# The end of attention re-ordered in a fused modulation, attention and feed-forward kernel: weight loads divided, first feed-forward sample moved a slot, first sample's values moved

## The reference, cut to what matters

```python
h = layernorm(x, gamma1, beta1)
Q, K, V = (h @ Wq + bq), (h @ Wk + bk), (h @ Wv + bv)      # 16 heads of 32
scores = einsum('bhqd,bhkd->bhqk', Q, K) / sqrt(32)        # causal mask, then softmax
x1 = x + softmax(scores) @ V @ Wo + bo
h2 = layernorm(x1, gamma2, beta2)
ff = gelu(h2 @ W1 + b1) @ W2 + b2                          # 512 -> 2048 -> 512
out = x + g * (x1 + ff - x)
```

## Time and profile before

| | |
|---|---|
| median of 3 runs | 1770.07 us (1762.8 to 1770.21) |
| the profiled execution's own time | 1769.55 us |
| its span | 1767.8 us |
| mean granted TensorE clock | 0.976 of full speed |
| TensorE busy | 1669.0 us, 94% of the span |
| VectorE / ScalarE / GpSimd busy | 66% / 56% / 24% |
| attention, slots 0 to 31 | about 278 to 1029 us of the span |

### The profile page before, as it was taken

The page is one execution under the profiler, slowest core; times in us unless marked ns, Lnnn a source line. Parts: engine busy times, 40 slices in busy tenths (PEclk is TensorE's granted clock), DMA queues, the critical chain, the costliest instruction groups (busy, mean ns, idle before and its releaser), DMA issues.

```text
span 1767.8 us, 27388 instructions
## 1 busy us (share of the span) xinstructions
PE 1669.0 (94%) x9384; PEld 1336.3 (76%) x9384; DVE 1174.1 (66%) x2758; ACT 986.7 (56%) x2289; POOL 420.2 (24%) x638
## 2 busy tenths in 40 slices
PE   5799997899999999999999879999999999999999
PEld 3688765667676767776676648888899999999998
DVE  5899776676676767676766555867665656565643
ACT  4788743777676766776667573634343434342422
POOL 6688520313131221313131122010101010101010
PEclk8999998899999999999999989999999999999999
DMA  6122233333434434343333713486646464646451
GB/s 281 72 95 75 94 116 99 97 96 96 106 94 112 105 83 117 97 120 83 93 96 73 240 54 110 160 302 263 249 167 239 167 247 163 259 166 255 162 197 66
DMA packets 61827, 254.82 MB, mean 144 GB/s; under 512 B 10580, under 2 KB 15956, under 8 KB 45944
## 3 DMA queue, kind: packets, MB, share of 16 engines
q1 hardware_dynamic: 61688, 253.06, 43.8%
HBM read 153.93 MB, written 48.23 MB: 114 GB/s over the span
## 4 chain that ended last, share of the span: by engine, by line
PE 72%; DVE 12%; ACT 6%; DMA 4%; SPq 3%; issue 2%; POOL 1%; DVEq 0%; ACTq 0%; POOLq 0%
PE psum L82 20%; PE psum L83 19%; PE psum L84 19%; PE psum L1616 3%; PE psum L1599 3%; PE psum L1644 3%; DVE psum L1147 2%; ACT psum L1384 2%; DMA k_stack<-k_maxima 1%; SPq L914 1%; ACT k_exps L1394 1%; SPq L922 1%; DMA k_stack<-k_samples 1%; ACT k_samples L1411 1%; DVE k_samples L1188 1%
## 5 line engine op out<-in xcount | busy, mean ns | idle before, releaser
L1384 ACT ACTIVATE psum<-psum,b_mx 128x512 f32<-128x512 f32 (+3 forms) x512 | 260.6, 511 | 227.0 <-DVE b_mx L1147 225.1
L1147 DVE CUSTOM_DVE_ANT_0 psum<-psum,b_mask 128x512 f32<-128x512 f32 (+3 forms) x512 | 247.8, 505 | 206.8 <-PE psum L1599 203.9
L2443 ACT ACTIVATE k_act<-k_stack_f,k_smalls 128x512 f32<-128x512 f32 x112 | 81.0, 723 | 336.1 <-DVE k_stack_f L2231 336.1
L1394 ACT ACTIVATE k_exps<-psum 128x512 f32<-128x512 f32 (+1 forms) x384 | 205.3, 536 | 10.8 <-PE psum L1616 10.8
L1616 PE MATMUL psum<-k_stack 98*128 98x512 f32 (+3 forms) x512 | 158.2, 351 | 32.7 <-ACT k_exps L1394 18.0
L2084 POOL TENSOR_SCALAR k_result<-k_result,k_pb 128x512 f32<-128x512 f32 x32 | 59.9, 1887 | 455.4 <-DVE k_result L2150 455.4
L2210 DVE TENSOR_TENSOR k_act_lo<-k_act,k_act_hi 128x512 fp32r<-128x512 f32 x112 | 77.4, 691 | 130.2 <-ACT k_act_hi L2446 130.1
L1599 PE MATMUL psum<-k_stack 96*128 96x512 f32 (+3 forms) x512 | 159.6, 354 | 1.4 <-ACT psum L1384 1.4
L82 PE MATMUL psum<-k_act_hi,k_w_hi 128*128 128x512 f32 x384 | 150.9, 393 | 1.0 <-DVE k_act_lo L2210 0.6
L83 PE MATMUL psum<-k_act_lo,k_w_hi 128*128 128x512 f32 x384 | 150.6, 392 | 0.0
L84 PE MATMUL psum<-k_act_hi,k_w_lo 128*128 128x512 f32 x384 | 150.3, 391 | 0.0
(11 more groups left out here) (365 smaller groups left out, 4568.9 us busy)
## 6 DMA issues: line engine op xcount, KB each, us to landing
k_stack<-w_factors SPq DMA_DIRECT2D x35, 1792.0 KB, 7.3
k_stack<-k_samples SPq DMA_DIRECT2D x384, 128.0 KB, 2.4
k_weights<-w_factors SPq DMA_DIRECT2D x17, 1792.0 KB, 7.8
x<-k_tokens SPq DMA_DIRECT2D x10, 1024.0 KB, 3.9
k_tokens<-x SPq DMA_DIRECT2D x8, 1024.0 KB, 4.8
d<-k_result SPq DMA_DIRECT2D x32, 256.0 KB, 2.5
k_raw<-x SPq DMA_DIRECT2D x8, 1024.0 KB, 4.8
k_raw<-d SPq DMA_DIRECT2D x8, 1024.0 KB, 6.9
```

The costliest lines, as they stand in the source:

```text
L1147: last = dve.tensor_tensor_reduce(got, got, mask[:, S - width:S], -INV_SQRT_DH, -2.0 * MASKED, ALU.add, ALU.min, mx[n % 2][:, h, t:t + 1])
L1384: act.activation(sc(n, u)[:, at:at + width], sc(n, u)[:, at:at + width], ACT.Exp, bias=mx[n % 2][:, h, t:t + 1], scale=-1.0, accum_out=sum ...
L1394: act.activation(exps[n % 2][:, h, at:at + width], by_key(n, u)[:, 0:width], ACT.Exp, scale=INV_SQRT_DH).then_inc(k_act, 1)
L2443: act.activation(act_f[:], whole_tile, ACT.Gelu, bias=small(smalls, "b1", 2 * pair % M + second)).then_inc(pair_gelu, 1)
```

## The change

It moves instructions between places of the lists; no instruction of the arithmetic is added or removed. In its parts:
1. **Values of sample 0.** The second half of its values (24 matmuls) goes from slot 1 to slot 0 (`values_in`). In slots 0 and 1 the first `maxima` stands at step 7, not 8, and `maxima_out` one step earlier too (`maxima_step`).
2. **Steering.** VectorE takes the four steering products at steps 5 and 6, two each, instead of three at step 6 and one at step 7.
3. **SyncE, every sample.** In slots with g = 0 and g = 1 the small copies of the maxima (`max_rows(n, 0)`) go ahead of the 1 MB store of the steered sample and of the 1 MB load of the next.
4. **SyncE, the last slots.** The loads of sample 0's `x` and `d` go from the end of slot 29 to two places in slot 30. The W1 and W2 loads of slot 30 go behind the maxima: W1's first half into slot 31, W2's quarter to the end of slot 31, W1's second half into slot 32.
5. **The first feed-forward sample.** `tokens_back`, the scaling and splitting, the weight splits and the first two `first_product` go from slots 32 (end) and 33 into slot 32; what follows moves a slot forward too. Four second products then stand ahead of the last output products of attention, which before lay between them. The additions for sample 0 are made at steps 2 and 3 of slot 31 instead of 0 to 3.

The core of the diff (left out: the steps of `split_low`, `scale_back` and of the later `step(m)`, which move in the same way):

```diff
+def maxima_step(n):
+    return 8 if n >= 2 else 7
 def values_in(n):
     b, g = divmod(n, G)
-    if n == -1:
-        return 0, V_TILES[0]
-    return b, (V_TILES[g] if present(b) and g < 2 and (b or g) else ())
+    if n in (-1, 0):
+        return 0, V_TILES[n + 1]
+    return b, (V_TILES[g] if present(b) and g < 2 and b else ())
...
         def slots(after):
...
+                if n == GROUPS - 2:
+                    first_after("x2")
+                if n in (GROUPS - 1, GROUPS):
+                    after("w1", n - GROUPS + 1)
                 if 0 <= n + 1 < GROUPS:
                     stack_rows(n + 1, (0, 1))
...
+                if g == 3 and present(b - 1):
+                    attention_out(b - 1, 3)
+                if 0 <= n < GROUPS:
+                    max_rows(n, 0)
+                if n == GROUPS - 2:
+                    first_after("d")
+                if n == GROUPS - 1:
+                    after("w2")
                 if g == 0 and present(b + 1):
                     steered_out(b + 1)
                 if g == 1 and present(b + 2):
                     sample_in(b + 2)
-                if n == GROUPS - 2:
-                    after("weights")
-                if g == 3 and present(b - 1):
-                    attention_out(b - 1, 3)
-                if 0 <= n < GROUPS:
-                    max_rows(n, 0)
...
-                if u == 6:
-                    for j in range(J - 1):
-                        steered(b + 1, j)
-                if u == 7:
-                    steered(b + 1, J - 1)
+                if u in (5, 6):
+                    steered(b + 1, 2 * (u - 5))
+                    steered(b + 1, 2 * (u - 5) + 1)
...
-            if n == GROUPS and u in (10, 11):
-                tokens_back(AFTER, 2 * (u - 10))
-                tokens_back(AFTER, 2 * (u - 10) + 1)
+            if n == GROUPS and u in (1, 2):
+                tokens_back(AFTER, 2 * (u - 1))
+                tokens_back(AFTER, 2 * (u - 1) + 1)
...
-            if (n, u) == (GROUPS + 1, 9):
+            if (n, u) == (GROUPS, 10):
                 gelu(0)
...
-            if (n, u) == (GROUPS + 1, 7):
+            if (n, u) == (GROUPS, 8):
                 first_product(0)
-            if (n, u) == (GROUPS + 1, 9):
+            if (n, u) == (GROUPS, 10):
                 first_product(1)
```

More of the change, by code:

```diff
@@ L766, in bank_uses @@
     if g == 0:
-        return qk + each("st", b + 1, range(J), "dve") + bc + v + after_back
+        return qk + after_back + each("st", b + 1, range(J), "dve") + bc + v
     if g == 1:
@@ L936, in attention_out, with first_after @@
             sp.dma_start(sample_at(io["d"], b)[:, j, :], d_out[:, j % 2, :]).then_inc(d_st[j % 2], 16)
-        def first_after():
-            wait_full(sp, ("v", B - 1, V_TILES[1][-1]))
-            sp.dma_start(first, sample_at(io["x2"], 0)).then_inc(sample_ld, 16)
-            for k in range(2):
-                sp.wait_ge(d_st[k], 16 * 2)
-            sp.dma_start(first_d, sample_at(io["d"], 0)).then_inc(sample_ld, 16)
+        def first_after(which):
+            if which == "x2":
+                wait_full(sp, ("v", B - 1, V_TILES[1][-1]))
+                sp.dma_start(first, sample_at(io["x2"], 0)).then_inc(sample_ld, 16)
+            else:
+                for k in range(2):
+                    sp.wait_ge(d_st[k], 16 * 2)
+                sp.dma_start(first_d, sample_at(io["d"], 0)).then_inc(sample_ld, 16)
         def slots(after):
@@ L1247, in beside @@
                 over_sums(n - 2)
-            if u == 9 and 0 <= n < GROUPS:
+            if u == maxima_step(n) + 1 and 0 <= n < GROUPS:
                 maxima_out(n, 0)
@@ L1281, in beside @@
             if n == GROUPS - 1:
-                if u < J:
-                    if u == 0:
+                if u in (2, 3):
+                    if u == 2:
                         dve.wait_ge(sample_ld, 32)
-                    dve.tensor_tensor(first[:, u, :], first[:, u, :], first_d[:, u, :], ALU.add).then_inc(mid_set, 1)
+                    for j in (2 * (u - 2), 2 * (u - 2) + 1):
+                        dve.tensor_tensor(first[:, j, :], first[:, j, :], first_d[:, j, :], ALU.add).then_inc(mid_set, 1)
                 if u in (6, 7):
@@ L1291, in beside @@
                     normalise(AFTER, 2 * (u - 9) + 1)
-            if n == GROUPS + 1 and u in (0, 1):
-                split_low(2 * u, AFTER)
-                split_low(2 * u + 1, AFTER)
+            if n == GROUPS and u in (3, 4):
+                split_low(2 * (u - 3), AFTER)
+                split_low(2 * (u - 3) + 1, AFTER)
         def ahead(place, part=None):
@@ L1460, in beside @@
                     tokens_out(AFTER, 2 * (u - 4) + 1)
-            if (n, u) in ((GROUPS, 11), (GROUPS + 1, 0)):
-                if u:
+            if n == GROUPS and u in (2, 3):
+                if u == 2:
                     wait_full(act, ("k", B - 1, G - 1))
                     wait_full(act, ("v", B - 1, V_TILES[1][-1]))
-                for j in (0, 1) if u else (2, 3):
+                for j in (2 * (u - 2), 2 * (u - 2) + 1):
                     scale_back(AFTER, j)
@@ L1789, in slots @@
                             context(n - 2, 2)
-                    if u == 8 and 0 <= n < GROUPS:
+                    if u == maxima_step(n) and 0 <= n < GROUPS:
                         maxima(n, 0)
@@ L1994, in sync, with after @@
     def sync(sp):
-        def after(at):
-            if at == "weights":
+        def after(at, n=None):
+            if at == "w1":
                 attention["projected"](sp)
-                for n in range(2):
-                    sp.dma_start(w1_raw[n], io["w1"][:, :, n * FF // 2:(n + 1) * FF // 2]).then_inc(w1_ld[n], 16)
-                    if n == 0:
-                        attention["split"](sp)
-                        sp.dma_start(w2_raw[0], io["w2"][:, 0:QUARTER, :]).then_inc(w2_ld[0], 16)
+                sp.dma_start(w1_raw[n], io["w1"][:, :, n * FF // 2:(n + 1) * FF // 2]).then_inc(w1_ld[n], 16)
+            if at == "w2":
+                attention["split"](sp)
+                sp.dma_start(w2_raw[0], io["w2"][:, 0:QUARTER, :]).then_inc(w2_ld[0], 16)
             if at == "places":
@@ L2323, in after @@
         def after(n, u):
[L2324 removed]
+            if (n, u) == (GROUPS, 5):
                 w1_low(0)
[L2326 removed]
+            if (n, u) == (GROUPS, 6):
                 w2_low(0)
[L2328 removed]
+            if (n, u) == (GROUPS, 8):
                 w1_low(1)
[L2330 removed]
+            if (n, u) == (GROUPS, 9):
                 w2_low(1)
[L2332 removed]
+            if (n, u) == (GROUPS, 11):
                 split(0)
[L2334 to L2335 removed]
+            if (n, u) in ((GROUPS + 1, 1), (GROUPS + 1, 9), (GROUPS + 1, 11), (GROUPS + 2, 1)):
+                step(((GROUPS + 1, 1), (GROUPS + 1, 9), (GROUPS + 1, 11), (GROUPS + 2, 1)).index((n, u)))
         def samples():
```

26 lines of the change are left out of this document (9 added, 17 removed).

## The result

The changed kernel takes **1793.57 us** (median of 4 runs, 1791.7 to 1794.81), the kernel before 1769.2 (4 runs). The ratio is 1.0145, with a 95% interval of 1.0119 to 1.0171: slower by 24 us, where 16 us faster were forecast. The profiled execution has a span of 1792.1 us, 24.3 more than before.

A forecast was written before the change was run, and what follows sets the result against it. TensorE, busy 94% of the span, was taken as the bound, so only idle and half-clock time could be won. Gains of 6.8 + 6.9 + 3.2 − 0.9 = 16.0 us from 1769.55 gave 1753.5, range 1747 to 1760.

The forecast's parts named there:

- Part 3 I cost at nothing: SyncE's order in every sample: earlier maxima copies only help, later stack loads never reach TensorE; cost 0 us.
- The 1 MB transfers stall VectorE: Rival on part 3: about 13 slots lose 0.7 us each through late stacks, 9 us, giving 1762.6; chance 0.10.
- A: Last slots, part 4: moved loads end TensorE's wait for maxima; 6.8 us gained, between 3 and 9.
- the new stall: Last slots: VectorE waits for stores of `k_result` behind the 1 MB load of `d`; 1.5 us lost, at most 5.3.
- the clock that I counted at 2.5: Slot 31, after the ended wait for maxima: TensorE's clock does not fall, 2.5 us gained, up to 3.3.
- B: Steering, part 2: waits at steering products vanish in six g = 0 slots; 6.9 us gained, between 2 and 9.
- The first rival: Steering gives nothing: another engine bounds the g = 0 slots and idle moves to other matmuls; 1760.4 us, chance 0.14.
- C: The start, part 1: values fill slot 0's idle time, slot 1 waits less; 3.2 us gained, between 0 and 5.5.
- D: Slot 32, part 5: earlier feed-forward is given back through ScalarE; 0.9 us lost, between 3 lost and 0.5 gained.
- the rival of a double price: ScalarE, slot 32: each additional table switch costs double its row, 2.6 us more, 1756.1; chance 0.08.
- The last rival: Slot 32: W1 or W2 loads come too late, delaying ScalarE, GpSimd's cut and context; 1779 us and more, chance 0.03.

The follow-up runs named there:

- e1: The changed kernel with part 3 alone undone, parts 1, 2, 4 and 5 kept: 1763.08 us, ratio 0.9948 to the kernel before.
- e3: The kernel before with part 3 alone, the 1 MB store and load behind the copies of the maxima: 1811.18 us, ratio 1.0221.
- e5: The changed kernel with parts 3 and 5 undone, parts 1, 2 and 4 kept: 1763.27 us, ratio 0.9956 to the kernel before.
- e10: The kernel before with part 4 alone, the moved loads of the last slots: 1770.02 us, ratio 0.9983.
- e8: The changed kernel with part 3 undone and the load of `d` issued behind slot 30's two stores: 1765.53 us, ratio 0.9966 to the kernel before.
- e4: The kernel before with part 2 alone, steering products taken two and two at steps 5 and 6: 1762.39 us, ratio 0.9936.
- e9: The kernel before with part 1 alone, sample 0's values and earlier first maxima: 1771.73 us, ratio 0.9986.
- e6: The changed kernel with part 3 undone and the first gelu behind the last exponentials by key: 1761.03 us, ratio 0.9945 to the kernel before.
- e7_products_behind: As e6, with both first products also behind the last scores by key on TensorE: 1761.10 us, ratio 0.9947 to the kernel before.

## Why the prediction was wrong

**The step that failed is "Part 3 I cost at nothing".** It measured some 30 us: 28.6 in slots 4 to 27 (9.4 with g = 1, 19.2 with g = 2, changed kernel less e1), and 31 from the first score to slot 32; alone on the kernel before (e3) 34 in the profiles. The rival "The 1 MB transfers stall VectorE" had the mechanism at a price of 9 and a chance of 0.10. Three things in its working were off.
- "The stacks aren't used until the next slot" looked at the side that is written. The wait is on the side that is read: VectorE cannot overwrite `k_samples` until the copies are out of it, and it comes to that in step 2 of the slot.
- The row, 13.2 us over 12 places, was read as cover ("none of which reaches TensorE as far as I saw"). A wait that already happens has no slack; in slot 6 it went from 0.54 to 4.23 us, and TensorE, which had 6.81 busy us of 7 there, stood 3.56.
- The time before was taken as if the load stood just ahead of the maxima. It was issued at 404.71, 4.9 us before the maxima were there. The list's order had given it idle time of the queue, and moving it by one place in the list moved it by 7.3 us.

**A, forecast −6.8, is between −0.4 and −1.4** (e5 and e10 by the marks, from the start of slot 30, with their scatter of 0.9). The wait of 5.84 for the maxima did go: from one slot's first product by key to the next on TensorE, slot 30 took 29.76 us before (976.58 to 1006.34) and takes 23.57 now (997.40 to 1020.97). But slot 31, counted so, went from 22.73 to 26.13, and to 26.77 in e10. The term that was mis-sized is the new stall, put at 1.5: VectorE waits 3.2 us, and 3.4 to 4.0 of the gain are lost. The 1 MB of `d` landed 6.1 us after its issue, where the forecast had taken 4.0, and the first store behind it took 6.47 us, against 2.5 in e8, where it stands ahead of the load. VectorE, then the chain, then TensorE in the changed kernel:

```profile
1025.25 0.75 DVE L1194 TENSOR_SCALAR k_result<-psum,k_smalls 128x512 f32<-128x512 f32 x1 [3.21 <-DMA d<-k_result]
```

```profile
1018.68 6.47 DMA d<-k_result
```

```profile
1023.44 0.38 PE L1626 MATMUL psum<-k_stack 98*128 98x256 f32 x1 [1.33 <-ACT k_exps L1404]
...
1028.37 0.50 PE L1626 MATMUL psum<-k_stack 98*128 98x512 f32 x1 [2.93 <-ACT k_exps L1404]
```

With the load behind the stores (e8) the wait only moves to the load. And the clock that I counted at 2.5 did not come back: TensorE still stands 1.33 and 2.93 us there, and from one reciprocal to the next slot 31 has a granted clock of 0.79, where it had 0.81 before. In e10, whose code from slot 32 on is that of the kernel before but for the places of the loads, the 56 us from the start of slot 32 have 0.86, against 0.90 before.

**B, forecast −6.9, measured −7.0** in the changed kernel by slots (−6.8 in e4). What weight loads of TensorE wait for these operations has gone from 9.6 us to

```profile
PEld psum L1542 <- DVE k_tokens L1209: 4.4, 8, 1.5
```

The mechanism was right. That the sum met the number to 0.1 is partly luck: it took the three waits of slot 12 for all six slots, and by slots the gain is 0.6 to 1.3 us in five and 2.5 in slot 12, the one where the clock had fallen to 0.57 and is now 1.00. The first rival, in which this gain would be nothing, did not occur.

**C, forecast −3.2, is 0** (e9). The values fill slot 0's gap and the wait at slot 1's start goes, as forecast, and not through the steering: e4 keeps 2.14 of the 2.49. But slot 1 is then held by ScalarE, as the text had feared for its second half, and gives all of it back.

**D, forecast +0.9, measured about +2** (e1 less e5, 1.9 with the scatter of 0.9). Context starts 25.8 us into slot 32 (1047.10 to 1072.87), where 23.1 had been worked out and 17.9 was the time before. ScalarE in slot 32 of the changed kernel, from its wait for the last scores on:

```profile
1065.73 0.60 ACT L1404 ACTIVATE k_exps<-psum 128x512 f32<-128x512 f32 x1 [2.15 <-PE psum L1626]
1066.35 1.28 ACT L2434 ACT_TABLE_LOAD   x1
1067.64 0.69 ACT L2434 ACTIVATE k_act<-psum,k_smalls 128x512 f32<-128x512 f32 x1
1068.36 0.63 ACT L2438 ACTIVATE k_act_hi<-k_act 128x512 fp32r<-128x512 f32 x1
1069.01 1.28 ACT L1404 ACT_TABLE_LOAD   x1
1070.31 0.87 ACT L1404 ACTIVATE k_exps<-psum 128x512 f32<-128x512 f32 x2
1071.19 1.28 ACT L2434 ACT_TABLE_LOAD   x1
```

and TensorE:

```profile
1072.87 2.84 PE L1654 MATMUL psum<-k_exps,k_result 128*32 128x512 f32 x16 [4.01 <-POOL k_exps L1025]
...
1077.67 0.47 PE L82 MATMUL psum<-k_act_hi,k_w_first 128*128 128x512 f32 x1 [0.17 <-issue]
```

The table loads are there as forecast, 1.28 us each, and on the path: ScalarE is busy 5.87 of the last 9 us and TensorE 4.96. What was not in the sum is the wait of 2.15 ahead of them: the last scores by key stand behind the first product's 12 matmuls on TensorE. The exponential behind a load starts at once (1069.01 + 1.28, 1070.31), and e6 took both switches and the gelu off the path for 2.8 us, where two switches at double price and the gelu would be 6.4, so the rival of a double price is out; the 1.38 us of draining that the page "ScalarE: Activation LUTs" of the Trainium skill adds in "What ACT_TABLE_LOAD costs" does not show in this trace.

The last 1.8 of the 24.3 us come later, from the 61st product on, where no instruction was moved: 613.2 us there against 611.4 before. The experiments have 611.5 to 613.6 in this stretch, so it may be scatter. In the changed kernel VectorE waits 1.64 us for a load of `d` at 1214.01; why it came late there stays open. The stretch ahead of attention, too, is 0.9 shorter without a change. The sum by profiles: −0.9 ahead of slot 0, +21.8 from there to slot 30, +1.7 to the 61st product, +1.8 after it.

```profile
1214.01 2.50 DVE L2147 TENSOR_TENSOR k_raw<-k_raw 128x512 f32<-128x512 f32 x4 [1.64 <-DMA k_raw<-d]
```

In terms of the forecast that is −1 for A, −7 for B, 0 for C, +2 for D and +30 for part 3, which with the scatter is the measured 24. The last rival, weights too late for slot 32, did not occur: ScalarE has no wait for a load of weights in slot 32.

## What to carry to other kernels

In a queue that is issued in order, look up when each issue really happens before you move it: a large transfer that seems to stand in the way of a small one may be filling the queue's idle time, and behind the small one it lands on whatever comes next. For each transfer ask for both ends, who needs what it writes and who may overwrite what it reads. A wait that is in the trace already, however short, has no slack, and a short wait with other engines queued behind it can cost more than its length: here 27.1 us more of waiting on VectorE cost 30.8, with 8.0 us more of busy time on TensorE for the same matmuls.

## What the hardware showed that was not expected

- Ahead of attention no kernel of this study differs, and yet the first score of slot 0 starts anywhere from 274.33 to 280.26 us (the rows are of e6_gelu_behind and e7_products_behind). That is 0.3% of the time, as much as the gains in question, so single us were read from marks inside the traces.

```profile
274.33 0.79 PE L1609 MATMUL psum<-k_stack 96*128 96x512 f32 x1
```

```profile
280.26 0.79 PE L1609 MATMUL psum<-k_stack 96*128 96x512 f32 x1
```

- A wait of 4.23 us of VectorE made its slot 5.8 us longer, 2.1 of it beyond what the wait grew by, with the granted clock at 0.63 in the 7 us behind it.
- Six copies of 128 KB, issued 0.47 to 4.12 us behind a load of 1 MB, took 5.9 us as a median and the last 6.54, against 2.5 with the load 7.85 us ahead of them. A store of 256 KB issued 0.43 us behind a load of 1 MB took 6.47 us, against 2.5 without it.
